# A gather loop with one of its two waits taken out: each part of eight gathers waits for its buffer, and no longer for the part in front of it

## What is computed

```python
x = x + attn0(layernorm(x)) * silu(moe8(layernorm(x)))        # layer 0
xn = layernorm(x)
s = attn1(xn)                                                   # layer 1
top_w, top_idx = top_k(sigmoid(xn @ router.T + bias), 8)        # 8 of 160 experts
top_w = top_w / (sum(top_w) + 1e-9) * 2.5
routed = sum over the 8 chosen e of top_w[e] * (silu(xn @ w_gate[e].T) @ w_down[e].T)
shared = silu(xn @ w_gate_shared.T) @ w_down_shared.T
x = x + s * silu(routed + shared)
```

## Time and profile before

| | |
|---|---|
| device time, median of 2 runs | 1481.55 us (1480.31 to 1482.79) |
| span of the profiled execution, first to last instruction | 1367.7 us |
| difference of the two | 113.85 us |
| TensorE busy in the span | 1160.1 us (85%) |
| VectorE busy | 936.1 us (68%) |
| ScalarE busy | 615.4 us (45%) |
| GpSimd busy | 550.4 us (40%) |
| of it the 256 gathers, L1201 | 259.6 us |
| idle of GpSimd before the gathers | 186.1 us |

### The profile page before, as it was taken

The page is one execution under the profiler, slowest core; times in us unless marked ns, Lnnn a source line. Parts: engine busy times, 40 slices in busy tenths (PEclk is TensorE's granted clock), DMA queues, the critical chain, the costliest instruction groups (busy, mean ns, idle before and its releaser), DMA issues. The chain is left out here.

```text
span 1367.7 us, 22150 instructions
## 1 busy us (share of the span) xinstructions
PE 1160.1 (85%) x6688; PEld 657.2 (48%) x6688; DVE 936.1 (68%) x2795; ACT 615.4 (45%) x1294; POOL 550.4 (40%) x606
## 2 busy tenths in 40 slices
PE   4999999998998999999989979799687977967811
PEld 2434344433443433434434347588476765756600
DVE  4546877868868858768758646070859669678784
ACT  1424234223233323233232247677686776766611
POOL 0000361351440550541622512344656565656565
PEclk9999999999999999999999999899798988989955
DMA  9952013013002012112139358876565746746522
GB/s 295 301 238 83 28 42 97 22 40 94 29 33 92 33 45 77 39 39 77 37 114 288 129 179 256 230 236 212 152 193 185 234 146 197 227 153 209 165 64 59
DMA packets 155818, 183.59 MB, mean 134 GB/s; under 512 B 16621, under 2 KB 104237, under 8 KB 155078
## 3 DMA queue, kind: packets, MB, share of 16 engines
q1 hardware_dynamic: 139334, 148.83, 33.8%
q0 software_dynamic: 16384, 33.59, 8.5%
HBM read 83.79 MB, written 98.57 MB: 133 GB/s over the span
## 5 line engine op out<-in xcount | busy, mean ns | idle before, releaser
L1201 POOL DMA_INDIRECT y<-y_rows,idxy x256 | 259.6, 1014 | 186.1 <-DMA y<-y_rows,idxy 81.7
L1165 POOL DMA_INDIRECT rows<-xn,idx x256 | 252.2, 985 | 88.0 <-issue 84.9
L1029 ACT ACTIVATE hs<-GY 128x512 f32<-128x512 f32 x176 | 104.9, 597 | 333.4 <-PE GY L780 333.3
L796 PE MATMUL ACC<-hs,wff 128*128 128x512 f32 x352 | 188.4, 624 | 0.0
L780 PE MATMUL GY<-xn0T,wff 128*128 128x512 f32 x352 | 185.8, 610 | 0.0
L1725 DVE SCALAR_TENSOR_TENSOR V<-y,w8all,V 128x128 f32<-128x128 f32 x232 | 82.5, 356 | 114.8 <-PE V L933 99.0
L1145 POOL TENSOR_TENSOR ppause<-neg_half 128x1 f32<-128x1 f32 x64 | 13.8, 215 | 342.7 <-DVE idx L1495 231.5
L830 PE MATMUL U<-ident,xg 128*128 128x128 f32 x576 | 98.2, 296 | 53.8 <-ACT xT L1045 50.4
L1552 DVE TENSOR_TENSOR hs<-hs,B 128x512 f32<-128x512 f32 x96 | 65.8, 685 | 65.7 <-PE B L786 34.9
L830 PEld LDWEIGHTS U<-ident,xg 128*128 128x128 f32 x576 | 69.3, 150 | 78.5 <-issue 63.8
L786 PE MATMUL B<-xw,wff 128*128 128x512 f32 (+2 forms) x304 | 102.8, 612 | 1.2 <-DVE hs L1552 0.7
(11 more groups left out here) (273 smaller groups left out, 2085.8 us busy)
## 6 DMA issues: line engine op xcount, KB each, us to landing
xg<-rows SPq DMA_DIRECT2D x144, 256.0 KB
y_rows<-ys SPq DMA_DIRECT2D x144, 256.0 KB
rows<-zero SPq DMA_DIRECT2D x2, 12288.0 KB, 47.0
rows<-zero SPq DMA_DIRECT2D x6, 2048.0 KB, 9.5
wd<-in_wd SPq DMA_DIRECT2D x1, 5120.0 KB, 24.4
wff<-in_w SPq DMA_DIRECT2D x3, 1408.0 KB, 9.4
rows<-xn,idx POOLq DMA_INDIRECT x256
y<-y_rows,idxy POOLq DMA_INDIRECT x256
```

The costliest lines, as they stand in the source:

```text
L796: nc.tensor.matmul(ACC[:, :], w2_0[:, v, :], hs[:, v % RH, :], start=(v == 0), stop=(v == U0 - 1))\
L1029: nc.scalar.activation(hs[:, u % RH, :], G[u % 2][:, :], ACT.Silu).then_inc(sem["silu_ready"], 1)
L1165: pool.indirect_dma_start(rows, bass.IndirectOffsetOnAxis(ap=idx[:, t * 8 + k:t * 8 + k + 1], axis=0), xn1[:, t, :], None)\
L1201: pool.indirect_dma_start(y8[:, i % RG, k, :], None, y_d[0:groups * Q * P, :], bass.IndirectOffsetOnAxis(ap=idxy[:, b, t * 8 + k:t * 8 + k ...
```

## The change

Two lines are taken out of GpSimd's program. The wait for a free buffer stays, as do the waits of VectorE for each part and the waits for the stored groups ahead of each batch.

```diff
@@ -1195,8 +1195,6 @@
                     i = b * T + t
                     if i >= RG:
                         pool.wait_ge(two["y8_used"], i - RG + 1)
-                    if i:
-                        pool.wait_ge(two[f"gath{(i - 1) % RG}"], 16 * TOPK1 * ((i - 1) // RG + 1))
                     for k in range(TOPK1):
                         pool.indirect_dma_start(y8[:, i % RG, k, :], None, y_d[0:groups * Q * P, :], bass.IndirectOffsetOnAxis(
                             ap=idxy[:, b, t * 8 + k:t * 8 + k + 1], axis=0)).then_inc(two[f"gath{i % RG}"], 16)
```

## The result

| | kernel before | changed kernel |
|---|---|---|
| device time, median of 2 runs | 1481.55 us (1480.31 to 1482.79) | 1556.74 us (1547.89 to 1565.59) |
| ratio | | 1.0522, 95% interval 1.0442 to 1.0602 |
| span of the profiled execution | 1367.7 us | 1563.8 us |
| device time of that same execution | not given | 1565.59 us |

The changed kernel is 5% slower; the prediction was a gain of 0.7%.

What follows compares the result with a forecast made beforehand. VectorE's own work and its loop through ScalarE and TensorE were taken to pace seven of eight batches; removing its two last-batch gather waits, 2.52 + 8.12 = 10.64 us, gave 1481.55 - 10.64 = 1470.9 us, range 1469 to 1473 (8 in 10: 1467 to 1478).

Steps and rivals of the forecast that it cites:

- The base of the sum: Whole kernel: the 113.85 us between profiled execution and two-run median stay, so 1481.55 - 10.64 = 1470.9 us.
- Everything up to part 27 ... worth nothing.: Gathers of all batches but the last: earlier by up to 5.47 us, nobody waits for them, no gain.
- wrong in kind: Sign of failure: gather issue much over 0.94 us, or weigh(6,0) after 1287 with ScalarE waiting over 2.0 us for stored groups.
- The last batch: VectorE's two gather waits before the last batch's third and fourth weighings, 2.52 and 8.12 us, vanish: gain 10.64 us.
- Landing was slow there: Argument for a rival: gathers beside last stores delay part 28's release; gain only 5.8 us; partial gain's chance 0.14.
- The slower rival: Gather traffic moves into the middle batches' stream and slows it; 8 us slower, 1489.5 us; chance of slower 0.05.
- 4.7 us of new delay per batch: Middle batches: delay needed in each of six, 1.8 us of it excess, to pass the 10.64 us gained.
- The rule that I had set beside it: At the last stores: store and gather each lose 1.2 us by taking turns; gain 10.6 to 9.8 us.
- 0.02 for slower: Whole kernel: chance that the measurement tells it slower, against 0.97 same and 0.01 faster; about 30 us needed to tell.

Runs made afterwards that it cites:

- c_before: The kernel before, unchanged, profiled again beside the changed kernel on one of the four slower chips; 1483.21 us, 0.9964.
- pause: Kernel before with each landing wait replaced by a GpSimd power of 12 columns, 2.31 us, that the next part waits for; 1480.33 us, 0.9968.
- c_after: The changed kernel again, both landing waits out, on the same chip as the kernel before measured anew; 1567.66 us, 1.055.
- last_only: Kernel before with the landing wait left out in the last batch only; 1493.86 us, 1.0094.
- plain2: Changed kernel with plain transfers of 128 successive rows in place of the second stage's gathers, on a slower chip; 1414.25 us, 0.9545.
- combo: Kernel before, landing waits replaced by a 4-column GpSimd power ahead of each part and, except in the last batch, after its fourth gather; 1426.82 us, 0.9642.
- four: Kernel before with an extra landing wait after the fourth gather of each part; 1481.43 us, 0.9948.
- bench: Separate small kernel without the computation: TensorE and ScalarE take turns beside idle GpSimd, gathers, spaced gathers, plain DMAs or powers; 0.84 us a turn.

## Why the prediction was wrong, point by point

- **The base of the sum.** "The profiled execution lies 113.85 us below the median of the two runs; I keep this difference." This is the first step that failed. In every other profile here 1.8 to 2.1 us lie outside of the span. A gap of 114 us meant that the trace was of an execution under other conditions than the runs: on chip B the kernel before takes 1371.3 us. The waits that the sum took off were therefore not those of the runs: c_before, near the runs' time, waits for a gather once in the last batch, 4.52 us, and not 10.64. I had the number in hand and explained it away.
- **"Everything up to part 27 ... worth nothing."** The second step that failed, and the one that cost the sign. By the waits of the earlier trace rows it was sound: nobody waited for these gathers. But the gap that the landing wait made was worth something to TensorE and ScalarE, which wait for nothing of GpSimd's gathers: put back as a power of 2.31 us (pause), it brought the time back to 0.997. In the changed kernel a batch takes about 73 us, from 1266.33 to 1340.15 for two successive weigh(b,0); it was 54.96 for the same two in the trace of before, from 1125.10 to 1180.06. On one chip the seven distances from weigh(0,0) to weigh(7,0) sum to 436.7 us in c_before and 510.4 in c_after: 73.7 of the 79 us lie here, 10.5 a batch in the mean.
- **The mark for "wrong in kind" was half right.** I wrote: weigh(6,0) later than 1287 with ScalarE waiting on stored groups for longer than 2.0 us. weigh(6,0) came at 1483.84. ScalarE did wait, but with the releaser "remote", not for stored groups. A gather's issue stayed at 0.94 us, as I had expected.
- **The last batch.** The step itself held in kind. The last weighings of the changed kernel:

```profile
1545.88 3.10 DVE L1723 SCALAR_TENSOR_TENSOR V<-y,w8all,V 128x128 f32<-128x128 f32 x8 [18.25 <-remote]
...
1550.81 3.09 DVE L1723 SCALAR_TENSOR_TENSOR U<-y,w8all,U 128x128 f32<-128x128 f32 x8
1553.81 3.09 DVE L1723 SCALAR_TENSOR_TENSOR B<-y,w8all,B 128x128 f32<-128x128 f32 x8
...
1557.60 3.09 DVE L1723 SCALAR_TENSOR_TENSOR ACC<-y,w8all,ACC 128x128 f32<-128x128 f32 x8
```

  No gather wait is left, 10.64 us in the earlier trace rows. But weigh(7,0) stands still 18.25 us with the releaser "remote" instead of 8.08 for TensorE, ten more, which is as much as was won; last_only, with this edit alone, shows the same ten us and was not faster.
- **A reading.** "Landing was slow there, 5.47 us before part 27 against 2.2 to 2.3 elsewhere" leaves out part 26, with 4.91 us. Nothing in the sum hangs on it. The sums themselves come out as written.
- **The slower rival** had the right sign and the right victim, the stream of the middle batches, but the wrong mechanism (transfers delaying stores) and the wrong size: 8 us for 75. DMA traffic was lower, not higher (91 GB/s in the stretch of gathers). "4.7 us of new delay per batch" was taken to be the largest that the bytes could give; the delay didn't come from bytes. The rule that I had set beside it, of the Trainium skill, page "DMA: Bandwidth & Descriptors", section "SWDGE vs HWDGE vs iDMA" (what GpSimd issues and what SyncE issues feed different queues of a DMA engine, served in turn), was not what decided: plain2 leaves the same bytes in the same queue of the profile (q0, 33.59 MB with the scatters) and took 0.9545. What those queues do inside an engine no run here shows.
- **The chances.** 0.02 for slower came from the cases I could name. A trace that lies 114 us off the runs should have widened everything: 8% of the time was of unknown origin.

## What to carry to other kernels

Compare the span of the profiled execution with the runs first; where they differ by per cents, the trace is of another case, and waits that it doesn't show can rule the runs. A wait that nobody needs for its data can still be useful for the silence it makes: before taking it out, put something harmless of the same length in its place (pause) and see whether the time stays. Where GpSimd issues long trains of indirect DMAs beside a stream of small TensorE and ScalarE steps, look for "remote" releasers, and try an opening of about 1 us every four. It paid here on the chips with late signals; on the fifth there was nothing late to free.

## What the runs showed of the hardware

- The same program took 1371.3 us on one chip and 1480 to 1487 on four others, with equal times of single instructions. The difference shows as waits with the releaser "remote", none on the one, 62 behind 925 us in c_before and 49 in c_after on another; and as semaphore changes that the trace lacks, from the first gather on 9 of the engines' 1432 in the trace of before, 389 of 1433 in c_before.
- On the four, TensorE's signals came late beside indirect DMAs: by up to 3.2 and 3.5 us at runs of four gathers (combo, four), 7.4 and 11.4 at eight (pause, c_before), 26.4 at sixteen, 35.1 at up to 32 (c_after). They got through in bursts some 2 to 4.5 us after the start of a run's last gather. Beside plain transfers of the same size, none was late (plain2, 0.03 us at most), also in its one row of 32. Of ScalarE's recorded updates none was late, of VectorE's few and by up to 4.1 us. Why is not shown, nor whether the recording has a part in it. In a small kernel beside 24 gathers, three turns of TensorE and ScalarE took 1.41 to 2.13 us instead of 0.84 (bench).
- An opening of 1.35 us every four gathers gave 0.964, one of 2.6 us every eight 0.997, one of 0.50 us every eight 1.049, and one of 0.50 us ahead of every gather 0.999.
- The granted clock followed: 0.941 in the trace on record of before, 0.913 in c_before, 0.892 in c_after; in the 41 us of gathers in which TensorE worked 11.30 us it was 0.67, between the two levels. I read it as a result of the late signals first, through which some of the loss passes; no run parts the two.
